# Loading an adaLN modulation matrix: casting tile DMAs on POOL's queue, or f32 chunks on SyncE's queue with a VectorE cast

## What is computed

```python
mod = (_silu(L0_c) @ L0_wmod).reshape(L0_c.shape[0], 6, 1, -1)
sa, ca, ga, sb, cb, gb = (mod[:, 0], mod[:, 1], mod[:, 2], mod[:, 3], mod[:, 4], mod[:, 5])
...
h = _layernorm(x, axis=-1) * (1 + ca) + sa
x = x + ga * _L0_attn_ref(h, L0_attn_wq, L0_attn_wk, L0_attn_wv, L0_attn_wo)
h = _layernorm(x, axis=-1) * (1 + cb) + sb
x = x + gb * _L0_ffn_ref(h, L0_ffn_w1, L0_ffn_w2, L0_ffn_w3)
```

## Time and profile before

| what | value |
|---|---|
| median of 2 runs | 8192.14 us (8175.82 to 8208.46) |
| the profiled execution's own time | 8177.01 us |
| its span on the slowest core (core 1) | 8175.5 us |
| spans of the 8 cores | 8141.6 to 8175.5 us |
| PE busy | 3292.2 us (40%) |
| ACT busy | 3055.8 us (37%) |
| DVE busy | 2768.9 us (34%) |
| POOL busy | 51.5 us (1%) |

### The profile page before, as it was taken

How to read it: one execution, slowest core, us unless ns; L and a number is a source line. 1 busy time by engine, 2 the same in 40 slices (tenths; PEclk the granted TensorE clock), 3 DMA queues, 4 the chain that set the end, 5 groups by cost and what they waited for, 6 DMA issues and landing times.

```text
span 8175.5 us, 55199 instructions; the slowest of 8 cores (8141.6 to 8175.5 us)
## 1 busy us (share of the span) xinstructions
PE 3292.2 (40%) x12512; PEld 1320.0 (16%) x12512; DVE 2768.9 (34%) x3809; ACT 3055.8 (37%) x4011; POOL 51.5 (1%) x100
## 2 busy tenths in 40 slices
PE   2425453545345263006656655631111111254544
PEld 0102221222122021002222222210000000011111
DVE  3152121212121213772333333246666666411111
ACT  0033434343434212463333333325555555322222
POOL 0000000000000000000000000000000000000000
PEclk8757786878687676557777877765555555567777
DMA  9902424333433332002222222211010110233333
GB/s 150 152 16 81 125 82 125 99 113 93 115 111 97 106 88 75 29 3 90 81 82 88 85 81 88 86 47 32 31 35 31 35 31 31 72 103 106 103 106 105
DMA packets 391041, 656.16 MB, mean 80 GB/s; under 512 B 44547, under 2 KB 192006, under 8 KB 386560
## 3 DMA queue, kind: packets, MB, share of 16 engines
q1 hardware_dynamic: 376896, 560.35, 22.3%
q0 software_dynamic: 13824, 92.28, 6.8%
HBM read 693.97 MB, written 50.51 MB: 91 GB/s over the span
## 4 chain that ended last, share of the span: by engine, by line
ACT 24%; DVE 24%; DMA 22%; PE 13%; issue 9%; SPq 5%; DVEq 1%; ACTq 1%; POOLq 0%
DMA wfl<-w 13%; DVE sm L253 6%; ACT tmpb L247 6%; PE ps L1380 4%; ACT esb L790 4%; DMA rbc<-w 4%; PE ps L649 3%; DMA mring<-wmod 3%; PE ps L886 2%; DVE ternB L1151 2%; ACT sgntmp L1144 2%; ACT terntmp L1137 2%; ACT sgntmp L1141 2%; ACT sgntmp L1146 2%; SPq L1120 1%
## 5 line engine op out<-in xcount | busy, mean ns | idle before, releaser
L1380 PE MATMUL ps<-q3c,ternA 128*128 128x512 bf16 x2048 | 764.0, 551 | 1941.0 <-DVE ternA L1357 1941.0
L247 ACT ACTIVATE tmpb<-sm,consts 128x512 f32<-128x512 f32 x1120 | 808.4, 722 | 173.7 <-DVE sm L253 119.6
L253 DVE SCALAR_TENSOR_TENSOR sm<-tmpb,sm 128x512 f32<-128x512 f32 x1120 | 774.6, 692 | 206.1 <-ACT tmpb L247 134.6
L1168 PE MATMUL ps<-q,ternA 128*128 128x512 bf16 x2048 | 574.0, 450 | 357.9 <-DVE ternB L1151 357.9
L1380 PEld LDWEIGHTS ps<-q3c,ternA 128*128 128x128 bf16 x2048 | 255.3, 130 | 2449.7 <-issue 2401.0
L1349 ACT ACTIVATE terntmp<-wfl,wsc 128x512 f32<-128x512 f32 x256 | 184.7, 721 | 1149.2 <-DMA wfl<-w 1060.9
L1357 DVE TENSOR_TENSOR ternA<-terntmp,sgntmp 128x512 bf16<-128x512 f32 x256 | 177.3, 693 | 1196.4 <-ACT sgntmp L1354 1196.4
L779 PE MATMUL ps<-qsb,ksb 128*128 128x512 bf16 x512 | 210.3, 422 | 912.3 <-ACT esb L790 824.2
L1179 PE MATMUL ps<-q,ternB 128*128 128x512 bf16 x2048 | 452.5, 379 | 0.0
L1148 DVE TENSOR_TENSOR ternA<-terntmp,sgntmp 128x2048 bf16<-128x2048 f32 x64 | 146.7, 2293 | 824.0 <-ACT sgntmp L1141 772.9
L803 DVE COPY rows<-ps 1x512 f32<-1x512 f32 x32 | 21.7, 679 | 1107.6 <-PE ps L779 828.8
(11 more groups left out here) (200 smaller groups left out, 4401.1 us busy)
## 6 DMA issues: line engine op xcount, KB each, us to landing
wfl<-w SPq DMA_DIRECT2D x1024, 256.0 KB, 4.6
rbc<-w SPq DMA_DIRECT2D x256, 256.0 KB, 4.3
wfl<-w SPq DMA_DIRECT2D x512, 128.0 KB, 2.4
mring<-wmod POOLq DMA_DIRECT2D x24, 2048.0 KB, 18.9
q3c<-q3s SPq DMA_DIRECT2D x384, 128.0 KB, 2.2
xst<-x2s SPq DMA_DIRECT2D x32, 512.0 KB, 3.9
hs<-hch SPq DMA_DIRECT2D x128, 128.0 KB, 1.7
hch<-hs SPq DMA_DIRECT2D x128, 128.0 KB, 2.3
```

The costliest lines, as they stand in the source:

```text
L247: sws[j] = st("scalar", lambda e, ch=ch, src_u=src_u: e.activation(out=ch["bb"], in_=src_u, func=AF.Sign, bias=consts[:, 8:9]), waits=[(sV ...
L253: e.scalar_tensor_tensor(out=ch["tb"], in0=ch["bb"], scalar=-(k / 2.0), in1=src_u, op0=ALU.mult, op1=ALU.add),
L1168: e.matmul((psU0 if th == 0 else psU1)[:, 0:512], tA[:, kc * 128:(kc + 1) * 128], q12[:, kc * OWN + th * 512: kc * OWN + (th + 1) * 512], ...
L1380: tsl=tsl: e.matmul(psx[:, 0:512], tsl[:, di * 128:(di + 1) * 128], qsl[:, th * 512:(th + 1) * 512], start=(k3 == 0), stop=(k3 == NFC - 1)),
```

## The change

The tile DMAs on POOL's queue go. In their place SP loads each slice kc of each tile by itself: 128 x 512 f32 values (256 KB, 2 KB per partition) into one of two halves of a new staging tile `mstg` (f32, 128 x 1024). A DVE copy then casts the slice into the same place in `mring` as before. Each SP load waits for the DVE cast two slices earlier, which read the half that it overwrites. Each matmul waits for its own slice's cast. The semaphores `sST0` and `sST1` count the loads of the two halves. In addition the second weight load of the attention stage now waits for `cosT`, since it is no longer behind the modulation tiles in POOL's list and would otherwise overwrite `t_b`.

```diff
+    mstg = K.sb("mstg", [128, 1024], F32, KB(175))
...
     mod_mm_base = sMM.n
-    for j in range(24):
-        st("gpsimd", lambda e, j=j: e.dma_start(
-            out=mring[:, (j % 2) * NKC * 512:((j % 2) + 1) * NKC * 512], in_=wmod_d[j]),
-           waits=[(sMM, mod_mm_base + j - 1)] if j >= 2 else [],
-           inc=(sM0 if j % 2 == 0 else sM1), inck=16)
+    mod_cast = {}
     w_modtt = 0
     for j in range(24):
-        wld = 16 * (j // 2 + 1)
-        sMp = sM0 if j % 2 == 0 else sM1
         slot = mring[:, (j % 2) * NKC * 512:((j % 2) + 1) * NKC * 512]
+        for kc in range(NKC):
+            sST = sST0 if kc % 2 == 0 else sST1
+            stg = mstg[:, (kc % 2) * 512:(kc % 2 + 1) * 512]
+            st("sync", lambda e, j=j, kc=kc, stg=stg: e.dma_start(
+                out=stg, in_=wmod_d[j][:, kc, :]),
+               waits=[(sVE, mod_cast.get((j, kc - 2),
+                                         mod_cast.get((j - 1, NKC - 2 + kc), 0)))],
+               inc=sST, inck=16)
+            wst = sST.n
+            mod_cast[(j, kc)] = st("vector", lambda e, j=j, kc=kc, stg=stg:
+                                   e.tensor_copy(
+                out=mring[:, (j % 2) * NKC * 512 + kc * 512:
+                          (j % 2) * NKC * 512 + (kc + 1) * 512], in_=stg),
+                waits=[(sST, wst)] +
+                      ([(sMM, mod_mm_base + j - 1)] if (kc == 0 and j >= 2) else []))
         for kc in range(NKC):
             st("tensor", lambda e, kc=kc, slot=slot: e.matmul(
                 psE[:, :], smat[:, kc * 128:(kc + 1) * 128],
                 slot[:, kc * 512:(kc + 1) * 512],
                 start=(kc == 0), stop=(kc == NKC - 1)),
-               waits=(([(sMp, wld), (sVE, w_smat)] +
+               waits=([(sVE, mod_cast[(j, kc)])] if True else []) +
+                     (([(sVE, w_smat)] +
                        ([(sVE, w_modtt)] if j >= 1 else []))
                       if kc == 0 else []),
...
         wcred = [(sMM, ev_done[events[i - 2]])] if i >= 2 else []
+        if i == 1:
+            wcred = wcred + [(sSE, w_cos)]
```

More of the change, by code:

```diff
@@ L192, in build @@
     sM1 = K.sem("sM1")
+    sST0 = K.sem("sST0")
+    sST1 = K.sem("sST1")
     sB = [K.sem("sB%d" % i) for i in range(6)]
```

## The result

The changed kernel takes 8573.2 us (median of 11 runs, 8557.1 to 8632.3) against 8195.2 us for the kernel before (median of 10). The ratio is 1.0467, with a 95% interval of 1.0437 to 1.0496: about 380 us slower. The forecast of 8684 us had the sign and the stage right and was 111 us too high; the measured time is 3 us above the lower end of the range.

The account below looks back on a forecast made before the run. Bound: the modulation stage, almost pure loading. First cast ends at 90.53 us; 191 x 4.21, 0.9 and 2.55 us more end the stage at 898.1, +509.4; less 2.5, +506.9 on 8177.01 makes 8684 us; range 8570 to 8885.

Parts of the forecast that it names:

- The place and the sign: Modulation stage, 90 to 389 us, on the path: its lengthening moves the end equally, +509.4 us; slower 0.97.
- The mechanism: Modulation stage: two staging halves, each cycling through load and cast, 191 cycles long; DMA share from 0.98 to a third or half.
- The hand-over of 0.08 us and the cast of 0.43: Modulation stage, per cycle: 0.08 us from DVE's end to SP's issue, 0.43 us for the 128x512 cast.
- From the start of SP's issue to the consumer, 3.70 us: Modulation stage, each 256 KB load: 3.5 us to landing plus 0.2 to DVE's start; near bounds 3.45 and 4.7.
- C: Modulation stage: cycle of one staging half, hand-over 0.08 plus load 3.70 plus cast 0.43, 4.21 us.
- the forecast's own case (0.77): Modulation stage: C of 3.6 to 5.0 us, giving 8567 to 8835 us; chance 0.77.
- Rival A: Modulation stage loads land as fast as 128 KB ones, 2.65 us to the consumer: C 3.16, 8483 us; chance 0.08.
- The cover at the tile borders: Modulation tile ends: 2.55 us through product and reduction hidden behind the next load, costed at nothing; at most 61 us.
- The distance g: Modulation stage: time between the two staging halves, about 0.9 us; nothing lost at tile borders below 1.2.
- The 2.5 us from the first bounce: First layernorm bounce read: attention weight loads, now issued in the first 90 us, no longer in its way; -2.5 us.
- The rule of the Trainium skill: DMA landing as 2.0 us plus bytes over 436 GB/s: 2.60 us for 256 KB, about 8512 us; not adopted.
- Rival C: SP's 384 loads: DMA engines, not the round trip, set the pace; stage 399 us, time 8277 us; chance 0.02.

Follow-up runs that it names:

- one_source_row: Changed kernel, but each staged load reads one 2 KB DRAM row for all 128 partitions instead of 128 rows; 8649.4 us (one run).
- six_slots: Changed kernel with six staging slots of 128x512 in place of two; 8268.5 us, ratio 1.0088 to the kernel before.
- late_product: Changed kernel with each tile's product and reduction on DVE moved behind the next tile's second cast; 8526.8 us, ratio 1.0435 to the kernel before.

## Why the prediction was right, and where it was off

*The place and the sign.* Right. The stage is on the path from end to end, and its 401 us appear in the time but for the scatter of the rest. The rest of the span (end minus gate, mean of the cores) is 7773 us in the profile before and 7752 in the one after; over the experiments on the changed kernel it is 7769 to 7786 in the three whose gate comes before 612 us, and 7734 to 7755 in the four others. One of the prediction's own signs of being wrong, a stage behind 900 us that changes its length by more than a few us, was thus met. The stretch from L1168 to L1380 (L1183 to L1395 after) is 29.6 us shorter, 1867.2 against 1837.6 us in the mean of the cores, and on all eight of them (1862.5 to 1876.0 before, 1831.5 to 1842.4 after); the stretch from L779 to L886 is 14 us longer. The first of them takes 1833 to 1858 us in all experiments on the changed kernel, in no order of the length of the modulation stage, and 1866 to 1867 in the edits of the kernel before. With one profile of each kernel that points to something in the changed kernel other than the stage's length; what it is stays open.

*The mechanism.* Right: two halves, each in a cycle of load and cast, 191 of them, DMA share down by half. One, four and six slots follow it: (landing + 0.20 + 0.43 + 0.08) over the number of slots, with the measured medians of landing, gives 3.31 us a slice for one slot, 1.18 for four and 0.92 for six, against 3.32, 1.20 and 0.99.

*The hand-over of 0.08 us and the cast of 0.43.* Right: the cast is 427 ns, and in the trace after SP's issue at 124.98 starts 0.07 us behind the end of the cast of 124.48.

*From the start of SP's issue to the consumer, 3.70 us.* This term of the sum was mis-sized: it is 2.81 us alone and, by the mean round of 3.47, 2.96 beside a second load (3.47 - 0.43 - 0.08; 2.87 in the second tile). C was 3.47 (3.466) and not 4.21: 0.744 us over 191 cycles, 142 us. It also lies below the 3.6 from which the forecast's own case (0.77) started. Both rows that I had taken it from carry something of their own. The bounce reads fetch one row 128 times (one_source_row shows that this is slower, 3.3 against 2.7 us). The scale loads come up to six at a time, 1.5 MB in flight, and six_slots has 4.8 us for that; that this also made the first of a pair slow is argued and not shown. I had written off the 128 KB loads as "the far bound"; at 2.65 us they were the nearest of all. Rival A, C of 3.16, was the better reading of this term.

*The cover at the tile borders.* This step failed. It cost the product and the reduction at nothing, as the data was to come 3.78 us after the cast; with 2.96 + 0.08 = 3.04 it is there before DVE is free, and 0.96 us are lost per border in the mean. At the border shown the halves are 118.18 - 116.70 = 1.48 us apart, so DVE is free only 1.48 + 2.55 = 4.03 us after the first half's cast. The two halves also do not stay close: after 121.17 and 121.95 they are 0.78 us apart, then 0.86, 1.33 and in the mean of the rest 1.4, so each border delays the first half anew. The distance g thus grows back to 1.4 in every tile, above the 1.2 that the prediction gave as the limit; it had said that the delay does not come back. late_product took 26.6 us back, within the 61 that I had given as the bound.

*The 2.5 us from the first bounce.* Not borne out as a term: on core 5 the same pair in the kernel before was 2.7 us apart and in the changed one is 4.0. It differs from core to core.

*The sum, corrected.* 8684 - 142 + 23 x 0.96 = 8564 us, against the profiled execution's own 8557.1. The stage comes out within 2 us: 509.4 - 142 + 22 = 389 us, against 779.4 - 388.9 = 390.5 between the gates of the two slowest cores. The 7 us that are left are the rest of the span, which is 10.5 us shorter on these two cores.

*How near a miss it was.* That the time falls into the range is in part luck. With C at 3.47 and every other term as forecast it would have been 8542 us, under the lower end of 8570; the profiled execution lies under it too. The borders, costed at nothing, gave 22 us back, and the median of the runs is 16 us above the profiled execution.

*The rule of the Trainium skill.* Its 2.60 us to landing for 256 KB was nearer (2.6 alone, 2.7 in pairs) than the rows that I preferred to it, and the time worked out from it, 8512 us, lies 45 us under the profiled execution; it leaves out the borders, 22 us, as well.

*Rival C, that bandwidth sets the pace.* Refuted for two slots (DMA share 0.51, one slot halves the pace), and it comes true in part with six.

## What to carry to other kernels

Replacing a few large DMAs by many small ones behind a small ring turns a bandwidth-bound stretch into a chain of round trips: time = number of loads / slots x (issue to landing + consumer + hand-over). Take the landing from a load of the same source pattern and the same bytes in flight, since a broadcast read (0.4 to 0.6 us) or a crowded queue (2 us with six in flight) is slower. With the landings measured here this formula falls short of the stage by 0 to 7%, as borders and the like are not in it. And where a stretch is bare loading, ask first which later stretch has idle DMA engines: moving two thirds of the tiles there gained 2.1%, where every staged version stayed slower than the kernel before.

## What the hardware showed that I had not expected

Reading one 2 KB DRAM row for 128 partitions lands 0.6 us later in the median (3.3 against 2.7) than reading 128 rows of 2 KB. Landing stays at 2.1 to 2.7 us up to 0.5 MB in flight and then grows by 1.3 to 1.7 us for the next 0.5 MB. A 256 KB read that was issued 5 us behind a casting load of 2 MB on another queue, with a second one 0.5 us behind it, reached its consumer only after 20.9 us. And PE's granted clock stood at 1.00 throughout the changed stage, in which PE had one matmul at a time with a wait in front, while it was 0.71 in the stage before, in which 16 came in a row; no time hung on it here. With four slots it was 1.00 as well (100 to 550 us), with six 0.61 (120 to 450 us).
